# A graph layer with a mixture of experts: router and experts in one block, late buffers over the node rows, one semaphore per gathered tile

## The chip, the cores and the metric

The kernel runs on one core of a Trainium2 chip. The metric is the device time of one execution in microseconds (us), the median of several runs. The core's engines each run their own instruction stream and meet at semaphores: TensorE (PE) multiplies matrices, VectorE (DVE) and ScalarE (ACT) work on elements, GpSimd (POOL) does elementwise work and issues the DMAs whose rows are addressed by an index (gathers and scattered stores), and SyncE (SP) issues the other DMAs.

## The reference

6250 nodes of 256 features, 200,000 edges, 8 experts with a hidden width of 1024.

```python
xn = layernorm(x)
x = x + relu(gcn(xn, src, dst)) + linear_attention_block(xn)
h = layernorm(x)
probs = softmax(h @ gate_w + gate_b)
idx = argmax(probs)                     # one expert a node
pos = rank of the node among those of its expert, in node order
kept = pos < 977                        # capacity ceil(1.25 * 6250 / 8)
y = relu(h @ w1[idx] + b1[idx]) @ w2[idx] + b2[idx]
x = x + nan_to_num(y * prob * kept, nan=0, posinf=1e4, neginf=-1e4)
```

## The kernel before

The program is a sequence of blocks; each engine has one stream per block, and all engines meet in a barrier between two blocks.

1. `prepare` and `aggregate_and_mix`: the normalisation, the products with the graph weights, the gathering of one row an edge through GpSimd, the attention and its feed-forward part. The node rows end in two buffers in SBUF, `acc` (49 blocks of 128 nodes, 260 columns) and `res` (49 blocks, 256 columns).
2. `route`: adds the two parts (`x2` on VectorE), scales the sum on ACT into `res` (`scale`), computes mean and variance of each row, the logits of the gate on TensorE (`transposes`, `logits`), the best expert, the place in it (`places`) and, by a product of one-hot matrices (`owners`), the node that owns each of the 8 x 8 x 128 slots. The 49 blocks go in five groups, `RB = [0, 12, 24, 36, 44, 49]`. While VectorE works on the blocks of one group, it does the steps of the group before in the gaps between blocks; `steps` says which step lies in which gap (`normal`, `choose`, `counted`, `probability`, `assign`). ACT does `copy`, `root`, `exponent` and `scale`. SP stores, for each group, the rows with four more columns (`rows_out` to `node_features`) and the plain rows to the output (`x2_out`), and waits for all of these at the end.
3. `experts`: eight experts, each with 977 slots, in `RT = 8` tiles of 128 rows, the last of 81. All weights and activations are split in a high part and a rest (`w1h`, `w1l`, `bTh`, `bTl`, ...), and each product is three products.

One expert in `experts` has two phases. In the **first phase** TensorE makes, for each of the `FT = 8` pieces of the hidden width and for each half of the rows, six matmuls `e_f` (L1837) in one of four PSUM banks. ACT writes the bias and the relu into `hbuf` (L1785), VectorE splits that into `hTh` (L1903) and `hTl` (L1905) and reduces w2 to its rest. In the **second phase** TensorE makes, for each tile t of rows, the two transposes `e_t` of tile t of the *next* expert (L1823) and then 24 matmuls `e_y` (L1850). Behind them, for tile t:

- VectorE adds the bias (`yb`, L1929), ACT multiplies by the probability (`yv`, L1800);
- VectorE in `classify`: `low`, `big`, `finite` (L1918 to L1920), which stand for -1e4, +1e4 and "is a number";
- GpSimd adds `low` and `big` (L1738);
- VectorE in `result`: `copy_predicated` puts `yv` over `low` where it's finite (L1893), waits until the store of tile t-2 has landed, since `oo` has two buffers, and then makes `oo` = `rows` times a column + `low` (L1896);
- GpSimd stores `oo` to its nodes (L1730).

VectorE runs `result(t-2)` and `classify(t-1)` behind `yb` of tile t; the last two tiles' results fall around the end of the phase, `result(7)` behind piece 1 of the next expert's first phase. GpSimd's stream is written out like this:

```python
pool.wait_ge(inf_ok, (e * RT + t) * 2 + 2)
nc.gpsimd.tensor_tensor(low[...], low[...], big[...], ALU.add).then_inc(pool_st, 1)
if t > 0:
    store(e, t - 1)
...
store(e, RT - 1)
if e + 2 < EXP:
    load_rows(e + 2)
```

`load_rows` (L1714) issues eight gathers, one a tile, into one of the two buffers of `rows`. ACT normalises the gathered rows (`normalise`, L1759, output `xe`), tile 0 of the next expert at the last but one piece of the first phase. There `wait_rows` waits on one semaphore for the eight gathers of the buffer together. ACT copies the transposed rows (`bTh`, L1767) and VectorE takes the rest (`bTl`). SP loads w1 of the next expert (L1687) once `w1l` is done, and w2 (L1690) once `w2l` is. Experts 2 to 5 run in a hardware loop of two turns, the others are written out.

## Time and profile before

| | |
|---|---|
| median of 3 runs | 3107.11 us (3103.48 to 3110.45) |
| profiled execution | 3119.13 us |
| its span in the profile | 3117.4 us |
| mean granted clock of TensorE, share of full speed | 0.708 |
| TensorE matmul (PE) busy | 1802.9 us, 58% |
| VectorE (DVE) busy | 1236.0 us, 40% |
| ScalarE (ACT) busy | 802.9 us, 26% |
| GpSimd (POOL) busy | 1744.9 us, 56% |

Most of the span belongs to the aggregation, in which GpSimd issues 1563 gathers of edge rows. So these shares are averages over stages with different limits, and say little about the last 570 us, which the change touches. There the stretches have to be read by themselves: a row of the windows gives the busy time of each engine in one stretch; a row of a timeline gives one instruction with its start, its duration, its output and inputs, and in brackets how long its engine stood idle before it and what released it. "issue" there means that nothing shown in the profile was waited for. Of a matmul group or a pair of transposes the timeline's start is that of the first one.

### The profile page before, as it was taken

How to read it: one execution, taken by the hardware profiler on the slowest of the kernel's cores; microseconds unless marked ns; L12 is line 12 of the kernel's file. 1: busy time of each engine (PE TensorE's matmuls, PEld its weight loads, DVE VectorE, ACT ScalarE, POOL GpSimd, SP SyncE). 2: the span in 40 equal slices, each digit the busy share in tenths (PEclk: the TensorE clock that was granted, in tenths of full speed). 3: DMA queues.
4: the chain of work that ended last, by engine and by line, in shares of the span. 5: the costliest groups of instructions: out<-in, count | busy, mean ns of one | idle time of the engine just before them, and what ended most of it. 6: DMA issues, size and time to landing. Idle time of an engine off the chain costs nothing. (4 is left out here: it accounts for less than half of the span.)

```text
span 3117.4 us, 35225 instructions
## 1 busy us (share of the span) xinstructions
PE 1802.9 (58%) x8976; PEld 1564.4 (50%) x8976; DVE 1236.0 (40%) x3292; ACT 802.9 (26%) x1561; POOL 1744.9 (56%) x1844
## 2 busy tenths in 40 slices
PE   3745666645555555655555555555533356878978
PEld 2634444434444454544545445444422255778867
DVE  3522322233433334333343333434322247666756
ACT  1411212212222222222322222222100014544433
POOL 5055555666666666666666666666666630444544
PEclk6867888866666666666666666666666555889989
DMA  6366666666666665656556565666666635322220
GB/s 177 130 206 203 208 203 171 170 182 173 176 178 178 172 172 168 180 169 173 167 168 180 168 173 168 179 181 177 172 184 184 183 108 165 114 74 57 69 76 12
DMA packets 185241, 495.17 MB, mean 159 GB/s; under 512 B 34488, under 2 KB 66068, under 8 KB 184938
## 3 DMA queue, kind: packets, MB, share of 16 engines
q0 software_dynamic: 133008, 426.42, 47.8%
q1 hardware_dynamic: 52058, 66.62, 6.5%
q8 instruction: 85, 1.39, 0.2%
q14 instruction: 90, 0.74, 0.1%
HBM read 461.89 MB, written 33.79 MB: 159 GB/s over the span
## 5 line engine op out<-in xcount | busy, mean ns | idle before, releaser
L762 POOL DMA_INDIRECT ring<-node_rows,src_chunk x1563 | 1482.1, 948 | 954.5 <-SPq L741 448.7
L800 PE MATMUL p_item<-ring,sel 128*128 x3512 | 848.0, 393 | 727.6 <-DVE acc L1047 483.9
L800 PEld LDWEIGHTS p_item<-ring,sel 128*128 128x128 f32 x3512 | 692.1, 276 | 827.6 <-issue 825.1
L1047 DVE TENSOR_TENSOR acc<-acc,p_item 128x256 f32 (+1 forms) x439 | 183.6, 418 | 586.4 <-remote 454.7
L1028 DVE SCALAR_TENSOR_TENSOR sel<-dst_chunk,nbase,p_col 128x512 fp32r<-128x512 f32 x439 | 325.7, 742 | 63.9 <-issue 55.5
L840 PE MATMUL p_g<-x1T,w1t_sb 128*128 128x128 f32 x392 | 100.7, 438 | 173.6 <-ACT x1T L953 137.0
L1052 DVE SCALAR_TENSOR_TENSOR kf<-p_q,ke 128x256 f32<-128x256 f32 x49 | 20.8, 425 | 444.9 <-ACT ke L986 381.8
L840 PEld LDWEIGHTS p_g<-x1T,w1t_sb 128*128 128x128 f32 x392 | 86.7, 326 | 188.0 <-ACT x1T L953 148.4
L1738 POOL TENSOR_TENSOR low<-low,big 128x256 f32<-128x256 f32 x64 | 65.1, 1018 | 200.3 <-DVE big L1919 200.3
L1850 PE MATMUL e_y<-w2h,hTh 128*128 128x256 f32 x512 | 153.6, 300 | 0.2 <-DVE hTl L1905 0.2
L1850 PE MATMUL e_y<-w2l,hTh 128*128 128x256 f32 x512 | 147.9, 289 | 0.0
L1850 PE MATMUL e_y<-w2h,hTl 128*128 128x256 f32 x512 | 147.6, 288 | 0.0
L1714 POOL DMA_INDIRECT rows<-node_features,slot_row x64 | 68.9, 1077 | 120.3 <-POOLq L1199 101.2
L953 ACT ACTIVATE x1T<-p_t,col_ln1b,col_ln1g 128x128 f32<-128x128 f32 x98 | 39.5, 453 | 304.7 <-remote 285.2
L867 PE MATMUL p_q<-wq_sb,xnT_m 128*128 128x512 f32 x196 | 109.2, 685 | 8.4 <-ACT xnT_m L930 8.4
L860 PE MATMUL p_t<-ident,xn_m 128*128 128x128 f32 x98 | 26.0, 356 | 150.2 <-ACT xn_m L926 108.1
L1501 ACT COPY xT_r<-r_t 128x512 f32<-128x512 f32 (+1 forms) x25 | 14.3, 574 | 353.0 <-PE r_t L1548 352.9
L1850 PEld LDWEIGHTS e_y<-w2h,hTh 128*128 128x128 f32 x512 | 102.1, 199 | 0.7 <-DVE hTl L1905 0.6
L1850 PEld LDWEIGHTS e_y<-w2l,hTh 128*128 128x128 f32 x512 | 102.0, 199 | 0.0
L1850 PEld LDWEIGHTS e_y<-w2h,hTl 128*128 128x128 f32 x512 | 101.5, 198 | 0.0
L1125 DVE SCALAR_TENSOR_TENSOR kf<-p_q,ke 128x256 f32<-128x256 f32 x49 | 20.8, 424 | 200.3 <-ACT ke L939 101.1
L1837 PE MATMUL e_f<-bTh,w1h 128*128 128x490 f32 (+1 forms) x256 | 99.2, 387 | 1.7 <-issue 1.7
(258 smaller groups left out, 3167.4 us busy)
## 6 DMA issues: line engine op xcount, KB each, us to landing
ring<-node_rows,src_chunk POOLq DMA_INDIRECT x1563
self_rows<-node_rows SPq DMA_DIRECT2D x49, 256.0 KB
node_rows<-halves SPq DMA_DIRECT2D x11, 1024.0 KB, 4.3
w1raw<-in_w SPq DMA_DIRECT2D x8, 1024.0 KB
w2raw<-in_w SPq DMA_DIRECT2D x8, 1024.0 KB
res<-in_x SPq DMA_DIRECT2D x7, 896.0 KB, 7.9
node_features<-acc SPq DMA_DIRECT2D x3, 1560.0 KB, 6.2
out_dram<-res SPq DMA_DIRECT2D x3, 1536.0 KB, 10.9
```

What stands on the lines that cost most here:

```text
L762: nc.gpsimd.indirect_dma_start(ring[:, c % RING // U, c % U, :], None, table, bass.IndirectOffsetOnAxis(src_chunk[:, c:c + 1], 0)).then_in ...
L800: mm = pe.matmul(p_item[i % PSLOT][:, 0:C], sel[:, i % SELR, u, :], rows[:, u, h * C:(h + 1) * C].bitcast(F32R), start=(u == 0 and h == 0) ...
L840: mm = pe.matmul(p_g[:, m, :], w1t_sb[:, a, m * P:(m + 1) * P], x1T[:, a, :], start=(a == 0), stop=(a == CH - 1))
L860: mm = pe.transpose(p_t[:, a, :], xn[:, a * P:(a + 1) * P], ident[:])
L867: mm = pe.matmul(p_kv, xnT[:, a, :], wq_sb[:, a, C:3 * C], start=(a == 0), stop=(a == CH - 1))
L953: nc.scalar.activation(x1T[:, a, :], p_t[:, a, :], ACT.Identity, scale=g["cols"]["ln1g"][:, a:a + 1], bias=g["cols"]["ln1b"][:, a:a + 1]). ...
L1028: nc.vector.scalar_tensor_tensor(sel[:, i % SELR, :, :], dst.rearrange("p (u e) -> p u e", e=1).broadcast_to([P, U, P]), nbase[:, bass.ds( ...
L1047: nc.vector.tensor_tensor(a, a, p_item[j % PSLOT][:, 0:C], ALU.add).then_inc(added, 1)
L1714: nc.gpsimd.indirect_dma_start(rows[0:r, e % 2, t, :], None, feats, bass.IndirectOffsetOnAxis(slot_row[0:r, k:k + 1], 0)).then_inc(gathere ...
L1738: nc.gpsimd.tensor_tensor(low[0:r, t % 2, :], low[0:r, t % 2, :], big[0:r, t % 2, :], ALU.add).then_inc(pool_st, 1)
L1837: mm = pe.matmul(p_f[c % 4][:, 0:NH[h]], w[:, a, j * P:(j + 1) * P], b[:, a, h * NH[0]:h * NH[0] + NH[h]], start=(q == 0), stop=(q == len( ...
L1850: mm = pe.matmul(p_y[t % 2][:, 0:C], h[:, j, t * P:(t + 1) * P], w[:, j, :], start=(q == 0), stop=(q == len(parts) - 1))
```

## The change

- `route` and `experts` become one function, `tail`, with one block and no barrier between them. The buffers that the experts need late (`hTh`, `hTl`, `w2h`, `w2l`, `hbuf`, `finite`, `low`, `big`, `total`, `oo`) are put over `acc` and `res` in SBUF, the other ones have a place of their own. The PSUM banks of the router are those of the experts.
- The scaled rows in `res` are what is stored to `node_features`, with three further columns in place of four: `acc` is no longer multiplied again in the experts. The group's rows now wait for `scale` as well. SP issues the loads of expert 0's w1, w2 and the bias at the start of the block, and `x2_out` of a group directly behind its `rows_out`. The casts of expert 0's w1 (`high_w1`, `low_w1`) are done within routing. `root` of a group stands ahead of the group's last `copy`, steps of VectorE lie in other gaps, and `const3` is waited for later.
- Each gathered tile of rows has its own semaphore (`gathered[t]` for even experts, `arrived[t]` for odd ones), and `normalise` waits for its own tile.
- `oo` = `low` + `rows` is now a second addition on GpSimd, behind a wait for the landing of the store of tile t-2. VectorE makes `total` = `yv` + `rows` in `classify` and copies it over `oo` where it is finite; behind that the tile is stored.
- One semaphore fewer in the attention (`t_rec`), and strides of `res` and `acc` by the new widths.

```diff
-ROW = C + 4
+ROW = C + 3
...
+        nodes_at = nc.sbuf_base
+        acc = sb("acc", [P, NBLK, C])
+        res = sb("res", [P, NBLK, ROW])
+        nodes_end = nc.sbuf_base
...
-            acc = sb("acc", [P, NBLK, ROW], st=mid)
-            res = sb("res", [P, NBLK, C], st=mid)
...
-            route(nc, sb, ps, sem, locals())
-        experts(nc, sb, ps, sem, locals())
+        tail(nc, sb, ps, sem, locals())
...
+        over = [g["nodes_at"]]
+        def late(name, shape, dt=F32):
+            at = -(-over[0] // 32) * 32
+            over[0] = at + 4 * int(np.prod(shape[1:]))
+            assert over[0] <= g["nodes_end"]
+            return nc.alloc_sbuf_tensor_at(name, shape, dt, offset=at)
+        hTh, hTl = late("hTh", [P, FT, RT * P], F32R), late("hTl", [P, FT, RT * P], F32R)
+        w2h, w2l = late("w2h", [P, FT, C], F32R), late("w2l", [P, FT, C], F32R)
+        hbuf = late("hbuf", [P, 2, CAPE])
+        finite = late("finite", [P, 2, C], I32)
+        low, big = late("low", [P, 2, C]), late("big", [P, 2, C])
+        total, oo = late("total", [P, 2, C]), late("oo", [P, 2, C])
...
+        p_l, p_in, p_map = p_f[0:2], p_f[2:4], p_y[0]
...
+        arrived = [sem(f"arrived{t}", st) for t in range(RT)]
...
+        def wait_rows(eng, e, u, t):
+            if u == 0:
+                wait_apart(eng, gathered[t], rows_gathered(t) + e * 8 + 16, dma_fb, 32)
+            else:
+                wait_apart(eng, arrived[t], e * 8 + 8, dma_fb, 32)
...
+            def rows_out(gi):
+                sp.wait_ge(cols_ok, 3 * gi + 3)
+                sp.wait_ge(scaled, RB[gi + 1])
+                sp.dma_start(feats[RB[gi] * P:RB[gi + 1] * P, :].rearrange("(b p) c -> p b c", p=P),
+                             res[:, blocks(gi), :]).then_inc(dma_out, 16)
...
+            load_w1(sp, 0)
+            load_w2(sp, 0)
+            sp.dma_start(fb2_b[:].rearrange("p e c -> p (e c)"),
+                         fb2.rearrange("(a e) c -> a (e c)", a=1).broadcast_to([P, EXP * C])).then_inc(dma_fb, 16)
+            for gi in range(NG):
+                rows_out(gi)
+                x2_out(gi)
...
-            for gi in range(NG):
-                rows_out(gi)
-                if gi > 0:
-                    x2_out(gi - 1)
-            x2_out(NG - 1)
-            sp.wait_ge(dma_out, 16 * NOUT)
...
+            def load_rows(e):
+                for t in range(RT):
+                    r, k = nrows(t), e * RT + t
+                    nc.gpsimd.indirect_dma_start(
+                        rows[0:r, e % 2, t, :], None, feats, bass.IndirectOffsetOnAxis(slot_row[0:r, k:k + 1], 0)
+                        ).then_inc((gathered if e % 2 == 0 else arrived)[t], 16)
+            pool.wait_ge(slots_ok, 2)
+            pool.wait_ge(dma_out, 16 * NOUT)
...
+                pool.wait_ge(o_ok, k + 1)
...
+                    pool.wait_ge(inf_ok, T * 2 + 2)
+                    nc.gpsimd.tensor_tensor(low[0:r, t % 2, :], low[0:r, t % 2, :], big[0:r, t % 2, :], ALU.add
+                                            ).then_inc(pool_st, 1)
+                    pool.wait_ge(pool_st, T * 2 + 1)
+                    wait(pool, sent[t % 2], T // 2 * 16)
+                    nc.gpsimd.tensor_tensor(oo[0:r, t % 2, :], low[0:r, t % 2, :], rows[0:r, e % 2, t, 0:C], ALU.add
+                                            ).then_inc(pool_st, 1)
+                    if t > 0:
+                        store(e, t - 1)
+                store(e, RT - 1)
+                if e + 2 < EXP:
+                    load_rows(e + 2)
...
-                    V.scalar_tensor_tensor(acc[:, w, C], mv[:, :, 0], -1.0, r, ALU.mult, ALU.mult
+                    V.scalar_tensor_tensor(res[:, w, C], mv[:, :, 0], -1.0, r, ALU.mult, ALU.mult
                                            ).then_inc(cols_ok, 1)
+                    V.tensor_tensor(res[:, w, C + 1], r, sqd[:, w], ALU.mult).then_inc(cols_ok, 1)
...
+                    v.wait_ge(const3, 9)
...
-                for i, k in enumerate((0, 4, 4, 5, 5, 6)):
+                for i, k in enumerate((0, 5, 5, 6, 6, 7)):
...
-                for i, k in enumerate((17, 17, 18, 18, 19, 20, 21, 22)):
+                for i, k in enumerate((20, 20, 21, 21, 22, 22, 23, 23)):
...
-            v.wait_ge(const3, 9)
-            chain(V.tensor_copy(acc[:, :, C + 3:C + 4].rearrange("p b a -> p (b a)"), dinv[:]))
...
+                    v.wait_ge(pool_st, T * 2 + 2)
+                else:
+                    both = v.to_reg(T * 2 + 2)
+                    v.wait_ge(dma_fb, 32)
+                    v.wait_ge(fin_ok, both)
+                    v.wait_ge(pool_st, both)
+                V.copy_predicated(oo[0:r, t % 2, :], finite[0:r, t % 2, :], total[0:r, t % 2, :]
+                                  ).then_inc(o_ok, 1)
...
+                    V.tensor_tensor(total[0:r, t % 2, :], yv[0:r, t % 2, :], rows[0:r, u, t, 0:C], ALU.add
+                                    ).then_inc(fin_ok, 1)
...
+                    if gi == 1 and u < PC:
+                        low_w1(0, u)
...
+                wait_rows(s, e, u, t)
...
+                    if i == len(pairs(gi)) - 1:
+                        root(gi)
                     copy(t)
                     if i == 1 and gi > 0:
                         exponent(gi - 1)
-                    if 1 <= t <= held:
+                    if t > 0:
                         scale(t - 1)
-            root(NG - 1)
+                    if gi == 0 and i in (3, 4):
+                        high_w1(0, 2 * i - 6)
...
+                if t > 0:
+                    high_rows(0, t - 1)
+            high_rows(0, RT - 1)
+            s.wait_ge(dma_fb, 32)
+            s.wait_ge(dma_out, 16 * NOUT)
+            all_experts(s, expert)
...
-                elif t == 0:
-                    wait_rows(s, e, u)
...
-                V.copy_predicated(low[0:r, t % 2, :], finite[0:r, t % 2, :], yv[0:r, t % 2, :]).then_inc(o_ok, 1)
-                wait_apart(v, o_ok, 2 * T + 1, dma_fb, 16)
-                wait_apart(v, sent[t % 2], (e * (RT // 2) + t // 2) * 16, dma_fb, 16)
-                V.scalar_tensor_tensor(oo[0:r, t % 2, :], rows[0:r, u, t, 0:C], rows[0:r, u, t, C + 3:C + 4],
-                                       low[0:r, t % 2, :], ALU.mult, ALU.add).then_inc(o_ok, 1)
```

## Rows read from the trace of the kernel before

**Rows 1.** Windows: length, busy PE, PEld, DVE, ACT, POOL, PEclk, DMA, GB/s

```profile
2547.00:2644.00 97.00, 71.43 (x400) 68.30 (x400) 77.29 (x299) 47.45 (x93) 0.32 (x2) 0.50 0.37 124
3023.00:3032.00 9.00, 0.13 (x2) 0.11 (x2) 0.88 (x1) 0.78 (x2) 2.40 (x3) 0.65 0.67 171
```

**Rows 2.** TensorE timeline, experts: start, duration, instruction, [wait before it]

```profile
2690.09 0.38 PE L1823 MATMUL e_t<-ident,xe 128*128 128x128 f32 x2
...
2743.74 0.66 PE L1823 MATMUL e_t<-ident,xe 128*128 128x128 f32 x2 [6.78 <-issue]
...
2943.41 0.39 PE L1837 MATMUL e_f<-bTh,w1h 128*128 128x490 f32 x1
...
2974.58 0.68 PE L1823 MATMUL e_t<-ident,xe 128*128 128x128 f32 x2 [9.73 <-ACT xe L1759]
...
3031.92 0.66 PE L1823 MATMUL e_t<-ident,xe 128*128 128x128 f32 x2 [8.87 <-issue]
```

**Rows 3.** Timeline of ACT, the same columns

```profile
2973.85 0.60 ACT L1759 ACTIVATE xe<-rows 128x256 f32<-128x256 f32 x1 [10.89 <-DMA rows<-node_features,slot_row]
```

**Rows 4.** Timeline of GpSimd, the same columns

```profile
2648.50 0.97 POOL L1714 DMA_INDIRECT rows<-node_features,slot_row  x1 [101.18 <-POOLq L1199]
...
2940.48 1.00 POOL L1730 DMA_INDIRECT out_dram<-oo,slot_node  x1 [0.16 <-issue]
2942.66 0.73 POOL L1738 TENSOR_TENSOR low<-low,big 128x256 f32<-128x256 f32 x1 [1.18 <-DVE big L1919]
...
2949.17 1.28 POOL L1738 TENSOR_TENSOR low<-low,big 81x256 f32<-81x256 f32 x1 [0.73 <-DVE big L1919]
...
2955.12 1.77 POOL L1730 DMA_INDIRECT out_dram<-oo,slot_node  x1 [2.76 <-DVE oo L1896]
2957.19 1.06 POOL L1714 DMA_INDIRECT rows<-node_features,slot_row  x1 [0.30 <-issue]
...
2967.23 0.98 POOL L1714 DMA_INDIRECT rows<-node_features,slot_row  x1 [0.31 <-issue]
...
2988.92 1.03 POOL L1730 DMA_INDIRECT out_dram<-oo,slot_node  x1 [0.17 <-issue]
...
3093.94 1.01 POOL L1730 DMA_INDIRECT out_dram<-oo,slot_node  x1 [2.15 <-DVE oo L1896]
...
3107.81 1.24 POOL L1730 DMA_INDIRECT out_dram<-oo,slot_node  x1 [0.16 <-issue]
...
3112.12 1.01 POOL L1730 DMA_INDIRECT out_dram<-oo,slot_node  x1 [0.57 <-issue]
```

**Rows 5.** Timeline of VectorE, the same columns

```profile
2547.35 0.21 DVE L1460 COPY acc<-dinv 128x49 f32<-128x49 f32 x1 [1.89 <-POOL node_hi L1262]
...
2945.57 0.49 DVE L1896 SCALAR_TENSOR_TENSOR oo<-rows,low 128x256 f32<-128x256 f32 x1 [1.17 <-DMA out_dram<-oo,slot_node]
...
2949.20 0.66 DVE L1903 CAST hTh<-hbuf 128x978 fp32r<-128x978 f32 x1
...
2993.15 0.48 DVE L1896 SCALAR_TENSOR_TENSOR oo<-rows,low 128x256 f32<-128x256 f32 x1 [0.27 <-DVE low L1893]
...
3110.73 0.48 DVE L1896 SCALAR_TENSOR_TENSOR oo<-rows,low 81x256 f32<-81x256 f32 x1
```

**Rows 6.** The chain that ended last, from 2974 us on: start, length, work

```profile
3001.77 21.28 PE e_f L1837 x96
...
3059.05 21.29 PE e_f L1837 x96
```

**Rows 7.** Timeline of SP's DMA queue, the columns of the timelines

```profile
2639.48 1.89 SPq L1275 DMA_DIRECT2D out_dram<-res  x2
...
2647.84 0.39 SPq L1687 DMA_DIRECT2D w1raw<-in_w  x1
...
2939.91 0.37 SPq L1687 DMA_DIRECT2D w1raw<-in_w  x1
```

More of the change, by code:

```diff
@@ new lines, in tail @@
+        hTh, hTl = late("hTh", [P, FT, RT * P], F32R), late("hTl", [P, FT, RT * P], F32R)
[4 more added lines that the diff above has]
+        total, oo = late("total", [P, 2, C]), late("oo", [P, 2, C])
+        p_t = [ps(f"e_t{i}", [P, 4, P], st) for i in range(2)]
+        p_f = [ps(f"e_f{i}", [P, 512], st) for i in range(4)]
@@ new lines, in tail @@
+        p_y = [ps(f"e_y{i}", [P, 512], st) for i in range(2)]
+        p_l, p_in, p_map = p_f[0:2], p_f[2:4], p_y[0]
+        (const3, mean_ps, centred, x2_ok, var_ok, std, cols_ok, turned, xT_ok, l_ps, dv, e_ok, e_act, oh_ok, cum, one_ok, mapped,
+         scaled, slots_ok) = (sem("r_" + n, st) for n in (
+            "const3", "mean", "centred", "x2", "var", "std", "cols", "turned", "xT", "lps", "dv", "e", "eact", "oh", "cum", "one",
+            "mapped", "scaled", "slots"))
+        d_w1, d_w2 = sem("d_w1", st), sem("d_w2", st)
@@ L1237, in route @@
+        arrived = [sem(f"arrived{t}", st) for t in range(RT)]
+        sent = [sem(f"e_sent{i}", st) for i in range(2)]
+        (xe_ok, tr_ok, bh_ok, bl_ok, f1_ps, r_ok, hi_ok, lo_ok, f2_ps, yb_ok, y_ok, pool_st, inf_ok, fin_ok, o_ok,
+         w1h_ok, w1l_ok, w2h_ok, w2l_ok) = (sem("e_" + n, st) for n in (
+            "xe", "tr", "bh", "bl", "f1", "r", "hi", "lo", "f2", "yb", "y", "pool", "inf", "fin", "o", "w1h", "w1l",
+            "w2h", "w2l"))
         block = st.enter_context(nc.Block())
@@ L1249, in blocks_of, with nrows, w1_piece, w2_piece @@
             return range(2 * t, min(2 * t + 2, NBLK))
+        def nrows(t):
+            return P if t < RT - 1 else LASTR
+        def w1_piece(w, q):
+            n = F * CH // PC
+            return w[:, q * n // F, q * n % F:q * n % F + n]
+        def w2_piece(w, q):
+            return w[:, q * FT // PC:(q + 1) * FT // PC, :]
+        def all_experts(eng, expert):
+            for e in range(2):
+                expert(e, e, True)
+            with eng.Fori(1, EXP // 2 - 1) as it:
+                for u in range(2):
+                    expert(it * 2 + u, u, True)
+            expert(EXP - 2, 0, True)
+            expert(EXP - 1, 1, False)
@@ new lines, in rows_gathered, with load_w1 @@
+        def rows_gathered(t):
+            units = range(t, NUNIT, RING // U) if t < RING // U else ()
+            return 16 * sum(min(U, NCHUNK - k * U) for k in units)
+        def wait_rows(eng, e, u, t):
[3 more added lines that the diff above has]
+                wait_apart(eng, arrived[t], e * 8 + 8, dma_fb, 32)
+        def load_w1(sp, e):
+            sp.dma_start(w1raw[:], w1[bass.ds(e, 1)].rearrange("e (k p) f -> p (e k) f", p=P)).then_inc(d_w1, 16)
@@ new lines, in _, with store @@
+            load_rows(1)
+            def store(e, t):
+                r, k = nrows(t), e * RT + t
+                pool.wait_ge(o_ok, k + 1)
+                nc.gpsimd.indirect_dma_start(
+                    out, bass.IndirectOffsetOnAxis(slot_node[0:r, k:k + 1], 0), oo[0:r, t % 2, :], None,
+                    bounds_check=N - 1, oob_is_err=False).then_inc(sent[t % 2], 16)
+            for e in range(EXP):
+                for t in range(RT):
+                    r = nrows(t)
+                    T = e * RT + t
+                    pool.wait_ge(inf_ok, T * 2 + 2)
[10 more added lines that the diff above has]
+                    load_rows(e + 2)
@@ L1285, in _ @@
+            for q in range(2):
+                pool.wait_ge(sent[q], 16 * EXP * RT // 2)
         @block.vector
@@ new lines, in high_rows, with high_w1, high_w2 @@
+            def high_rows(e, t):
+                r = nrows(t)
+                s.wait_ge(tr_ok, e * RT + t + 1)
+                nc.scalar.copy(bTh[:, :, t * P:t * P + r], p_t[t % 2][:, 0:CH, 0:r]).then_inc(bh_ok, 1)
+            def high_w1(e, q):
+                if q == 0:
+                    s.wait_ge(d_w1, e * 16 + 16)
+                nc.scalar.copy(w1_piece(w1h, q), w1_piece(w1raw, q)).then_inc(w1h_ok, 1)
+            def high_w2(e, q):
+                if q == 0:
+                    s.wait_ge(d_w2, e * 16 + 16)
+                    wait(s, f2_ps, e * RT)
+                nc.scalar.copy(w2_piece(w2h, q), w2_piece(w2raw, q)).then_inc(w2h_ok, 1)
@@ new lines, in expert @@
+            def expert(e, u, more):
+                for j in range(FT):
+                    for h in range(2):
+                        wait_apart(s, f1_ps, e * 2 * FT + 2 * j + h + 1, dma_fb, 32)
+                        wait_apart(s, lo_ok, e * FT + j - 1, dma_fb, 32)
+                        nc.scalar.activation(hbuf[:, j % 2, h * NH[0]:h * NH[0] + NH[h]],
+                                             p_f[(2 * j + h) % 4][:, 0:NH[h]], ACT.Relu,
+                                             bias=fb1_sb[:, bass.ds(e, 1), j]).then_inc(r_ok, 1)
+                    if 1 <= j < 1 + PC:
+                        high_w2(e, j - 1)
+                    if more and j == FT - 2:
+                        normalise(e + 1, 1 - u, 0)
+                for t in range(RT):
+                    r = nrows(t)
+                    if more:
+                        high_rows(e + 1, t)
+                        if t + 1 < RT:
+                            normalise(e + 1, 1 - u, t + 1)
+                    s.wait_ge(yb_ok, e * RT + t + 1)
+                    wait(s, o_ok, e * RT + t - 1)
+                    nc.scalar.activation(yv[0:r, t % 2, :], yb[0:r, t % 2, :], ACT.Identity,
+                                         scale=rows[0:r, u, t, C + 2:C + 3]).then_inc(y_ok, 1)
+                    if more and 1 <= t < 1 + PC:
+                        high_w1(e + 1, t - 1)
```

460 lines of the change are left out of this document (151 added, 309 removed).

## The prediction, made before the result was known

> **What bounds the kernel now.** I read the windows first, then TensorE's timeline, then those of ACT, GpSimd, VectorE and SP. The aggregation fills the first 2547 us; the diff leaves its order of work alone (one semaphore fewer in `attention`, other strides), so I give it no change. Routing takes about 97 us, and VectorE is its busiest engine with 77.3 of them [rows 1]. Then come the barrier, the first gather at 2648.50 [rows 4] and the experts, to the end.
>
> In `experts` TensorE sets the pace: per expert a first phase of 96 matmuls `e_f` (21.3 us [rows 6]) and a second of eight tiles of `e_y`. Call F the start of the second phase, its first `e_t`. F is 2690.09 for expert 0, 2743.74 for the next, 2974.58 for expert 5, 3031.92 for expert 6 [rows 2] and 3080.34 for expert 7 (3059.05 + 21.29 [rows 6]). Six periods from 2690.09 to 3031.92 are 57.0 us each; the seventh is 48.4. The six end in a wait of TensorE in front of `e_t`, 6.78 us in the first, 9.73 and 8.87 in the last two [rows 2]; the seventh has none, and the difference of 8.6 is its price. What is late? ACT's `normalise` of tile 0 waits 10.89 us for DMA `rows` [rows 3]. The chain behind it: `result(e,7)` on VectorE, the expert's last store at 2955.12, eight gathers from 2957.19 to 2967.23, and the landing, at 2973.85 (6.6 us after the last one's start) [rows 3, 4]. `normalise` of tile 0 waits on one semaphore for all eight. While TensorE stands still its granted clock falls, to a mean of 0.65 in that window [rows 1].
>
> **Part 1, a semaphore per gathered tile.** Tile 0's gather starts 10.04 us before tile 7's [rows 4]. With the same 6.6 it lands at 2963.8; `e_f` ended at 2974.58-9.73 = 2964.85. If nothing before it is later, the whole wait goes, 8.6 a period. The other tiles start some 1.4 us apart and are used 27.2/8 = 3.4 apart, so they aren't late.
>
> **Part 2, the second GpSimd addition.** Here the change gives back. Before, VectorE wrote `oo`, and the wait for the landing of store t-2 stood there, two tiles later and mostly covered. VectorE gets `total` in `classify` instead, an addition of the same size (0.48 [rows 5]), so its own sum stays. Now GpSimd does low(t), waits for `sent` (store t-2 landed), adds `oo`, starts store(t-1). Store t-2 is the instruction just ahead of low(t), so its landing lies wholly in a loop: a turn = landing, counted from the store's start, + addition 0.73 + gap 0.16 [rows 4]. A landing isn't shown, so it is bounded. VectorE was held until 2945.57, 5.09 after the store at 2940.48 [rows 4, 5], but SP had started a `w1raw` load 0.57 us before that store [rows 7]. In the last expert, where no load runs, `oo` went at 3110.73 without such a wait, 2.92 after the store at 3107.81: there it's at most 2.9. In the middle experts `oo`(2) went at 2993.15, 4.23 after store(0) at 2988.92, held by another thing [rows 4, 5]: at most 4.2. From below, a turn can't be shorter than its own work: low, `oo` and store, 0.73+0.73+1.03+gaps 0.5 = 3.0 [rows 4]. I take 2.9 for a quiet landing (turn 3.8), one of four like it in that expert, and 5.0 for the one store of an expert beside the `w1` load (turn 5.9).
>
> The Trainium skill, "DMA: Bandwidth & Descriptors" (the table of fixed and variable cost), puts a DMA at about 2.0 us and bytes/436e9: an estimate of 2.3 us for 128 KB, 3.3 with 1.0 of issue, so turns of 3.2 to 4.2; with the middle of it the sum would stay the same. No run here shows the split.
>
> One middle expert, from F. (VectorE's and ACT's small steps are 0.3 to 0.6 each, like those of [rows 3, 5].) Store(0) started at 2988.92 = F+14.3. Ahead of it VectorE loses `oo`, 0.48 and a gap of 0.27 [rows 5]; GpSimd gains 0.89: s0 = F+14.5, and the turns give s1 = 18.3, s2 = 22.1, s3 = 25.9, s4 = 31.8 (contended: the load starts about F+24), s5 = 35.6.
> - Second phase: `e_t`(7) needs `xe`(7), which ACT issues behind yv(5), result(3), oo(3); that is done at s2-0.2 = 21.9. With copy_predicated, yv, bTh and xe, 2.2 together: 24.1, and `e_y`(7) ends at 27.4. Before: 3001.77-2974.58 = 27.2 [rows 2, 6]. So +0.2.
> - First phase: ACT reaches `hbuf`(0) behind yv(7), result(5), oo(5), done at 31.6: 33.4. TensorE has filled its four banks at 27.4+5.3 = 32.7 and waits 0.7. VectorE reaches `hTh`(0) behind oo(6) = 35.4, copy_predicated and `classify`(7): 37.0, which is 9.6 after the phase began, against 5.8 before (2949.20-2943.41 [rows 2, 5]). `hTl`(0) is ready at 38.9, `hbuf` of j=2 at 39.8; TensorE wanted it at 38.7: 1.1. Afterwards the engines keep step as now. Sum +1.9: 23.2, end at 50.6.
> - Gathers: oo(7), store(6) and store(7) behind s5, at the slow rate of the first phase (addition 1.28, store 1.77 [rows 4]): first gather at about 43.6, landed at 50.2. No wait, with 0.4 us to spare.
>
> With VectorE's `hTl`(7) 0.4 behind, the period is 51.0 for 57.0: six times -6.0, **-36**. Expert 6 to 7 had no wait to lose: 48.4 becomes 49.5, **+1.1**. In the last expert the tiles end by the loop: store(0) was at F+13.6, of which 2.15 is a stray gap [rows 4], so s0 = F+12; six turns 22.8, result(7) and a clash 1.4, and the 5.3 from the last store's start to the end (3112.12 to 3117.4): 41.5 for 37.1, **+4.7** with part of the gap kept.
>
> **Part 3, one program.** The `const3` wait ahead of routing goes: VectorE idled 1.89 before 2547.35 [rows 5], **-1.4**. At the end of routing two `out_dram` stores went out from 2639.48 to 2641.4, SP got past the barrier at 2647.84 and GpSimd gathered at 2648.50 [rows 4, 7]. The store of group 3 now leaves earlier, the last one 1.9 us earlier, and no barrier stands behind it; GpSimd still waits for all of `dma_out`. First gather near 2645: **-3.5**. Expert 0's `w1`: SP issues three loads at its start, ACT gets four casts, VectorE four subtractions, 0.6 to 0.7 each, under routing, where VectorE idled 19.7 of 97 us [rows 1]; uncovered 5.2. `e_f` then doesn't wait for the last `w1l` piece: **-1.6**. `root` now stands ahead of the last copy of a group and holds it until the variances are ready; later gaps for `assign` may save VectorE its waits for TensorE. Both together 0, bounds -5 and +5.
>
> **Sum.** -6.5 - 36 + 1.1 + 4.7 = -36.7. The profiled execution took 3119.13 (span 3117.4 and 1.7 around it): 3082.4. The median of the runs was 3107.11, so 3070.
>
> **Rivals.**
> - The loop costs more, slower: quiet landing 4.2, turn 5.1, five such turns an expert, +6.5 us that all come through. Period 57.5: six times +0.5; seventh +9; last +13; front -4. Together +21: 3128. It decides from a landing of 3.9. For it: the distance of 4.23 in the middle experts excludes no less. Against: 2.92 in the last.
> - The loop is covered: landing 2.2 or less, turns near 3.1 to 3.6. Period 48.7, -50; front -13 with VectorE's waits gone; last +2: 3046.
> - Port clashes: low beside `hTh` and `hTl` took 1.28 for 0.73 [rows 4]. Five additions now fall in the first phase; if each stops VectorE for its 0.73, +3.6 an expert: the saving is 2.4 x 6, seventh +4.7, the rest as above, 3095. The Trainium skill, "SBUF — State Buffer" (Who interferes with whom), has a VectorE instruction with two SBUF inputs and a GpSimd one that reads SBUF block each other fully. By that rule, the stretched row agrees.
> - The change doesn't do what it says: tile 0 lands as late as tile 7, no wait goes; 3107 with a covered loop.
>
> **How the numbers follow.** Forecast 0.55 (3050 to 3088), slow loop 0.17, covered loop 0.13, clashes 0.11, nothing gained 0.04. The range 3042 to 3108 leaves out the slow loop and little more. A measurement of this kernel can tell about 0.2% from no change, 6.2 us. Faster 0.77, same 0.07, slower 0.16.
>
> **What would show it.** No 7 to 10 us ahead of `e_t` of tile 0, and no fallen clock there; GpSimd's `oo` addition waiting for DMA `out_dram`, released 2.9 after the store, once an expert near 5; copy_predicated waiting for GpSimd; 23 us of `e_f`. I am wrong if the landing isn't 2.9, or if first gathers come after F+46.

## The result

The changed kernel takes 3064.95 us (median of 4 runs, 3060.90 to 3071.16) where the kernel before took 3108.78 in the same runs: a ratio of 0.9861, 95% interval 0.9836 to 0.9886. That is 43.8 us less. The forecast was 3070, the range 3042 to 3108.

The profiled execution took 3060.90 us, its span is 3059.1 us: 58.3 less than the profile of before. Not all of this is the change's. The aggregation's last step on VectorE stands at 2545.04 us in the profile of before and here at

```profile
2533.93 0.42 DVE L1048 TENSOR_TENSOR acc<-acc,p_item 128x256 f32<-128x256 f32 x1 [0.46 <-PE p_item L801]
```

11.1 us earlier, in a stage that the change leaves alone. In the ten profiles of the experiments, whose kernels all share this stage, it stands anywhere from 2529.45 to 2549.33 in eight runs on two chips, and at 2104.5 and 2105.0 in two runs on a third. On the first two chips and here, its mean is 2538.6 us in the three profiles of kernels with the old routing and 2538.3 in the seven with the new one: it is scatter. So below I use **the tail**: the span less that time. It is 572.4 us before and 525.2 after, 47.2 less, close to what the medians say. For a single profile it tells more than the span.

TensorE's timeline of the changed kernel, the start of a second phase (the first `e_t`) for experts 0, 1, 5 and 6, as [rows 2]:

```profile
2667.28 0.38 PE L1892 MATMUL e_t<-ident,xe 128*128 128x128 f32 x2
...
2716.52 0.44 PE L1892 MATMUL e_t<-ident,xe 128*128 128x128 f32 x2 [0.30 <-DVE w2l L1603]
...
2917.79 0.43 PE L1892 MATMUL e_t<-ident,xe 128*128 128x128 f32 x2 [0.43 <-DVE w2l L1603]
...
2967.65 0.44 PE L1892 MATMUL e_t<-ident,xe 128*128 128x128 f32 x2 [0.36 <-DVE w2l L1603]
```

The waits of 6.78 to 9.73 us of [rows 2] are gone, 0.3 to 0.5 are left. Six periods take 50.06 us each ((2967.65-2667.28)/6). What the windows show of the granted clock behind the wait was not in my sum. Six microseconds of the second phase of experts 3, 4 and 5 before (the columns of [rows 1]; the sixth figure after the stretch's length is the granted clock):

```profile
2860.00:2866.00 6.00, 5.70 (x30) 5.71 (x31) 2.19 (x3) 2.04 (x5) 0.00 (x0) 0.56 0.01 3
2916.00:2922.00 6.00, 5.70 (x35) 5.71 (x36) 2.61 (x4) 2.10 (x6) 0.00 (x0) 0.68 0.00 0
2974.00:2980.00 6.00, 5.42 (x34) 5.42 (x35) 2.61 (x4) 2.33 (x5) 0.00 (x0) 0.68 0.00 0
```

and of the changed kernel, experts 3, 4 and 5:

```profile
2817.00:2823.00 6.00, 5.16 (x41) 4.96 (x42) 4.41 (x6) 1.85 (x5) 3.66 (x4) 1.00 0.95 244
2867.00:2873.00 6.00, 5.02 (x40) 4.74 (x40) 4.67 (x7) 1.82 (x5) 3.92 (x4) 1.00 0.87 263
2917.00:2923.00 6.00, 4.93 (x39) 4.38 (x38) 4.76 (x7) 2.00 (x4) 4.24 (x4) 1.00 0.77 154
```

Before, TensorE came out of its wait at half clock (1.2 GHz; behind the first wait the window 2743 to 2749 reads 0.50 throughout) and got the full 2.4 GHz only some microseconds later: 30 to 35 matmuls in 6 us in these three. Now the clock is at 1.00 at the start of every second phase, and TensorE does 39 to 41 in the same time although it still pauses for `hTl`. It falls once more, in the middle of expert 6's second phase (see the seventh period below).

GpSimd's timeline of the changed kernel, middle of expert 4, as [rows 4]:

```profile
2880.92 1.29 POOL L1391 DMA_INDIRECT out_dram<-oo,slot_node  x1 [0.17 <-issue]
...
2885.05 1.02 POOL L1391 DMA_INDIRECT out_dram<-oo,slot_node  x1 [0.16 <-issue]
2886.27 0.73 POOL L1400 TENSOR_TENSOR low<-low,big 128x256 f32<-128x256 f32 x1 [0.21 <-DVE big L1642]
2887.64 0.76 POOL L1404 TENSOR_TENSOR oo<-low,rows 128x256 f32<-128x256 f32 x1 [0.63 <-DMA out_dram<-oo,slot_node]
2888.56 1.00 POOL L1391 DMA_INDIRECT out_dram<-oo,slot_node  x1 [0.16 <-issue]
...
2892.14 1.00 POOL L1391 DMA_INDIRECT out_dram<-oo,slot_node  x1 [0.16 <-issue]
2893.35 0.73 POOL L1400 TENSOR_TENSOR low<-low,big 128x256 f32<-128x256 f32 x1 [0.21 <-DVE big L1642]
2897.00 0.74 POOL L1404 TENSOR_TENSOR oo<-low,rows 128x256 f32<-128x256 f32 x1 [2.92 <-DMA out_dram<-oo,slot_node]
2897.89 1.00 POOL L1391 DMA_INDIRECT out_dram<-oo,slot_node  x1 [0.15 <-issue]
...
2908.56 1.74 POOL L1391 DMA_INDIRECT out_dram<-oo,slot_node  x1 [2.19 <-DVE oo L1619]
2910.60 1.06 POOL L1374 DMA_INDIRECT rows<-node_features,slot_row  x1 [0.30 <-issue]
```

This is the loop of part 2. A quiet store lands 2.59 us after its start (2885.05 to 2887.64), a turn is 3.5 (2885.05 to 2888.56); the one of 2892.14, beside the `w1` load that SP starts 0.58 before it, lands after 4.86, its turn is 5.75. In the last expert the turns are 3.3 to 3.6. SP's queue:

```profile
2891.56 0.37 SPq L1320 DMA_DIRECT2D w1raw<-in_w  x1
```

### The profile page after: what moved, and what is told of

Its sections match the earlier page's. It is cut to its first block and busy times, and to the rows that moved or that the text cites. A ratio compares the mean times of both kernels' runs of the same rounds, so it can differ in the third digit from the quotient of the medians.

```text
span 3059.1 us, 35293 instructions
## 1 busy us (share of the span) xinstructions
PE 1785.2 (58%) x8976; PEld 1547.8 (51%) x8976; DVE 1256.7 (41%) x3296; ACT 798.5 (26%) x1561; POOL 1788.8 (58%) x1908
## 5 line engine op out<-in xcount | busy, mean ns | idle before, releaser
L801 PE MATMUL p_item<-ring,sel 128*128 x3512 | 837.3, 390 | 653.8 <-DVE acc L1048 454.5
L801 PEld LDWEIGHTS p_item<-ring,sel 128*128 128x128 f32 x3512 | 684.3, 273 | 750.4 <-issue 747.5
L1053 DVE SCALAR_TENSOR_TENSOR kf<-p_q,ke 128x256 f32<-128x256 f32 x49 | 20.8, 425 | 506.9 <-ACT ke L987 324.3
L841 PE MATMUL p_g<-x1T,w1t_sb 128*128 128x128 f32 x392 | 99.1, 433 | 164.4 <-ACT x1T L954 147.6
L819 PE MATMUL p_q<-xnT_m,wq_sb 128*128 128x128 f32 x392 | 80.3, 371 | 126.3 <-ACT xnT_m L980 124.2
L819 PEld LDWEIGHTS p_q<-xnT_m,wq_sb 128*128 128x128 f32 x392 | 72.5, 277 | 132.0 <-ACT xnT_m L980 128.1
L861 PE MATMUL p_t<-ident,xn_m 128*128 128x128 f32 x98 | 25.9, 354 | 149.1 <-ACT xn_m L927 106.9
L1400 POOL TENSOR_TENSOR low<-low,big 128x256 f32<-128x256 f32 x64 | 52.0, 812 | 82.7 <-DVE big L1642 82.2
L1906 PE MATMUL e_f<-bTl,w1h 128*128 128x490 f32 (+1 forms) x256 | 99.5, 388 | 0.0
```

What stands on the lines that cost most here:

```text
L801: mm = pe.matmul(p_item[i % PSLOT][:, 0:C], sel[:, i % SELR, u, :], rows[:, u, h * C:(h + 1) * C].bitcast(F32R), start=(u == 0 and h == 0) ...
L819: mm = pe.matmul(p_q[:, m, :], wq_sb[:, a, m * P:(m + 1) * P], xnT[:, a, :], start=(a == 0), stop=(a == CH - 1))
L841: mm = pe.matmul(p_g[:, m, :], w1t_sb[:, a, m * P:(m + 1) * P], x1T[:, a, :], start=(a == 0), stop=(a == CH - 1))
L1400: nc.gpsimd.tensor_tensor(low[0:r, t % 2, :], low[0:r, t % 2, :], big[0:r, t % 2, :], ALU.add).then_inc(pool_st, 1)
L1906: mm = pe.matmul(p_f[c % 4][:, 0:NH[h]], w[:, a, j * P:(j + 1) * P], b[:, a, h * NH[0]:h * NH[0] + NH[h]], start=(q == 0), stop=(q == len( ...
```

## The experiments

All times are medians against runs of the kernel before on the same chip; "tail" is from the profile, as above (before 572.4). Experiments 1 to 4 ran on one chip (the kernel before: 3108.41 us), 5 to 8 on a second (3111.22), 9 and 10 on a third (2679.18). The periods and tails are from one profile each.

**1. Part 1 alone.** The kernel before, with

```diff
-                        ).then_inc(gathered[t] if e == 0 else d_r[e % 2], 16)
+                        ).then_inc((gathered if e % 2 == 0 else arrived)[t], 16)
...
-                elif t == 0:
-                    wait_rows(s, e, u)
+                wait_rows(s, e, u, t)
```

> The kernel before with part 1 alone (a semaphore for each gathered tile, and the attention's two semaphores merged as in the change, to make room). Theory: the wait ahead of `e_t` cost more than its 8.6 us, since TensorE's granted clock stood at 0.57 for the first 6 us of the second phase behind it; without it the second phase is as short as that of expert 0 (25.5 us of `e_y` for 27.5) and the first keeps its 21.4. Periods of 47.0 us for 57.0, six of them, and the seventh 47 for 48.4: -61 in all, 3047 us, so faster than the changed kernel. Rival: tile 0's gather starts some 41 us behind the start of the second phase and lands 5 us later, when TensorE is already through: a wait of 1 to 2 us stays and the periods are 49, 3060.

Measured 3044.61 us against 3108.41, ratio 0.9782 (0.9758 to 0.9805); tail 512.5. Six periods of 47.2, the seventh 46.7, the last expert 36.2. TensorE doesn't wait, and the windows at the start of the second phases of experts 1 and 4:

```profile
2734.00:2740.00 6.00, 5.99 (x50) 5.70 (x49) 4.11 (x6) 2.71 (x6) 3.22 (x3) 1.00 0.86 257
...
2875.00:2881.00 6.00, 5.62 (x44) 5.20 (x43) 4.67 (x7) 2.04 (x4) 4.02 (x4) 1.00 0.88 264
```

The second phases of experts 1 to 6 take 155.7 us together, for 164.4 in the kernel before. A period is 9.75 shorter (56.97 and 47.22): 8.7/6 = 1.45 of it is the second phase behind the fallen clock, 8.3 the wait, for which I had read 8.6. One part of the change gives more than the whole of it. The rival's rest of a wait isn't there.

**2. Part 2 undone in the changed kernel.**

```diff
-                    wait(pool, sent[t % 2], T // 2 * 16)
-                    nc.gpsimd.tensor_tensor(oo[0:r, t % 2, :], low[0:r, t % 2, :], rows[0:r, e % 2, t, 0:C], ALU.add
-                                            ).then_inc(pool_st, 1)
...
-                V.copy_predicated(oo[0:r, t % 2, :], finite[0:r, t % 2, :], total[0:r, t % 2, :]
-                                  ).then_inc(o_ok, 1)
+                V.copy_predicated(low[0:r, t % 2, :], finite[0:r, t % 2, :], yv[0:r, t % 2, :]).then_inc(o_ok, 1)
+                wait_apart(v, o_ok, 2 * T + 1, dma_fb, 32)
+                wait_apart(v, sent[t % 2], (e * (RT // 2) + t // 2) * 16, dma_fb, 32)
+                V.tensor_tensor(oo[0:r, t % 2, :], rows[0:r, u, t, 0:C], low[0:r, t % 2, :], ALU.add).then_inc(o_ok, 1)
...
-                    V.tensor_tensor(total[0:r, t % 2, :], yv[0:r, t % 2, :], rows[0:r, u, t, 0:C], ALU.add
-                                    ).then_inc(fin_ok, 1)
```

> The changed kernel with part 2 undone: GpSimd adds only `low` and `big`, VectorE copies over `low` and adds `rows` into `oo` behind its own wait for the landing of the store of tile t-2. Theory (the loop on GpSimd costs 2 us of each first phase and 3.7 at the end): periods of 47 for 50, the last expert 37 for 40.8: 3 x 7 + 4 = 25 less than the changed kernel, 3040 us. Rival: the time behind the second phase is lost to the two engines' clashes in `hTh` and `hTl`, which VectorE's `oo` brings back in another form: 5 to 8 less, 3058.

Measured 3036.98 us, ratio 0.9761 (0.9737 to 0.9784); tail 500.1. It is the lowest median on this chip, with an interval that overlaps those of experiments 1 and 3. First phases 21.5, six periods 47.3, last expert 36.2. In the middle experts the chain that ended last now runs through TensorE; two of its pieces:

```profile
2795.16 21.35 PE e_f L1902 x96
...
2870.55 2.90 PE e_y L1915 x24
```

In the changed kernel the same chain goes through the landings of the stores, here in expert 4:

```profile
2885.05 2.46 DMA out_dram<-oo,slot_node
2888.56 2.44 DMA out_dram<-oo,slot_node
2892.14 4.72 DMA out_dram<-oo,slot_node
2897.89 2.38 DMA out_dram<-oo,slot_node
```

**3. Four buffers for `oo`.** GpSimd keeps both additions; it waits for the store four tiles back.

```diff
-                    wait(pool, sent[t % 2], T // 2 * 16)
+                    wait(pool, sent[t % 4], T // 4 * 16)
```

> The changed kernel with four buffers for `oo` and four `sent` semaphores (two pairs of others merged to make room): GpSimd still makes both additions, but waits for the store four tiles back. Theory (what costs is the landing in the loop): the turns fall from 3.5 and 5.75 us to TensorE's 3.1, the first phase goes from 23.6 to 22, the last expert from 40.8 to 38: 17 less than the changed kernel, 3048 us. Rival (what costs is GpSimd's second addition itself, and VectorE stopped beside it): turns as before but for the one beside the load, at most 5 less, 3060.

Measured 3040.41 us, ratio 0.9776 (0.9750 to 0.9802); tail 504.1. First phases 21.5, six periods 47.1, last expert 37.5. So the cost was the landing in the loop: with it out, the addition on GpSimd gives the same periods as that on VectorE (47.1 and 47.3), and I had expected too little of it (3048). Of the 4 us more in the tail than in experiment 2, 2.8 stand ahead of expert 0's second phase. GpSimd's timeline in the last expert has turns of 3.0 us (3023.59 to 3026.58), the lower end of my bound:

```profile
3023.59 1.25 POOL L1395 DMA_INDIRECT out_dram<-oo_b,slot_node  x1 [0.15 <-issue]
...
3026.58 1.24 POOL L1395 DMA_INDIRECT out_dram<-oo_a,slot_node  x1 [0.16 <-issue]
```

**4. The changed kernel again.**

> The changed kernel once more, on the chip of the others, as the measure for them: 3065 us. Its trace also shows how much the aggregation varies: its last step on VectorE ended 11.1 us earlier than in the kernel before, though the change alters nothing there but strides and one semaphore; I expect values spread over 10 us for either kernel.

Measured 3066.13 us, ratio 0.9866 (0.9840 to 0.9892); tail 525.9, periods 50.15, the aggregation's end at 2529.76. Experiment 2 is 29 us faster (26 in the tail): this is what part 2 costs. By the forecast's own terms it was 2.5 a period, 1.1 and 4.7, 21 in all; here it is 2.9 a period, 2.8 in the seventh and 5.3 in the last.

**5. Part 1 undone.** `normalise` of tile 0 waits for all eight tiles of its expert.

```diff
-                wait_rows(s, e, u, t)
+                if isinstance(e, int) and e == 0:
+                    wait_rows(s, e, u, t)
+                elif t == 0:
+                    for every in range(RT):
+                        wait_rows(s, e, u, every)
```

> The changed kernel with part 1 undone: `normalise` of tile 0 waits for the eight gathers (experts 1 to 7). Theory: the wait is back and longer than before the change, since the first gather starts 43.1 us behind the start of the second phase (before the change 40.9) and the last one 10 later: periods of 59.2 to 60 for 50.1, with a granted clock below 0.7 at the start of the second phase: 3120 to 3127 us, slower than the kernel before. Rival: the per-tile semaphores did nothing, the wait went by the rest of the change: 3065.

Measured 3129.65 us against 3111.22, ratio 1.0056 (1.0033 to 1.0080); tail 587.0. Periods of 59.9, as foretold, and a granted clock of 0.50 to 0.70 over the 6 us behind the waits; the time is 3 us above what I had expected. TensorE's timeline has the waits again, here those of experts 2 and 5; the second was 9.73 in [rows 2]:

```profile
2802.78 0.68 PE L1896 MATMUL e_t<-ident,xe 128*128 128x128 f32 x2 [9.79 <-ACT xe L1740]
...
2983.19 0.69 PE L1896 MATMUL e_t<-ident,xe 128*128 128x128 f32 x2 [10.57 <-ACT xe L1740]
```

**6. The next w1 loaded later**, when the stores of the second phase have gone out.

```diff
-                    sp.wait_ge(w1l_ok, e * PC + PC)
+                    if isinstance(e, int) and e == 0:
+                        sp.wait_ge(w1l_ok, PC)
+                    else:
+                        sp.wait_ge(o_ok, e * RT)
                     load_w1(sp, e + 1)
```

> The changed kernel with the load of the next w1 held until the last `copy_predicated` of the expert before (for experts 1 to 6), so that no store of the second phase runs beside it. Theory: the fifth turn of 5.75 us (landing 4.9) becomes 3.5 like the others, the stores from s4 on are 2.2 earlier, ACT reaches `hbuf` 2 us earlier: 1.5 a period, 10 us in all, 3055. Rival: that landing is long for another reason and the time doesn't move; or the load now meets the gathers and `xe` waits for them, then slower by 1 to 2 a period.

Measured 3057.64 us, ratio 0.9828 (0.9802 to 0.9855); tail 515.9, that is 10 less than in experiment 4 (525.9), periods of 48.4. (By the medians it is 8.5 less, with intervals that overlap a little.) GpSimd's timeline at the store that took 4.86 to land:

```profile
2893.91 1.00 POOL L1394 DMA_INDIRECT out_dram<-oo,slot_node  x1 [0.16 <-issue]
2895.12 0.73 POOL L1403 TENSOR_TENSOR low<-low,big 128x256 f32<-128x256 f32 x1 [0.21 <-DVE big L1645]
2896.48 0.74 POOL L1407 TENSOR_TENSOR oo<-low,rows 128x256 f32<-128x256 f32 x1 [0.64 <-DMA out_dram<-oo,slot_node]
```

2.57 us, like the others. The load beside it was the reason.

**7. The store ahead of the addition.** Two lines moved on GpSimd.

```diff
+                    if t > 0:
+                        store(e, t - 1)
                     pool.wait_ge(pool_st, T * 2 + 1)
                     wait(pool, sent[t % 2], T // 2 * 16)
                     nc.gpsimd.tensor_tensor(oo[0:r, t % 2, :], low[0:r, t % 2, :], rows[0:r, e % 2, t, 0:C], ALU.add
                                             ).then_inc(pool_st, 1)
-                    if t > 0:
-                        store(e, t - 1)
```

> The changed kernel with one line moved on GpSimd: store(t-1) is started ahead of the wait for store(t-2) and of the addition `oo`(t). The landing now has two turns' time. Theory (a loop through both engines): the store's 1.0 us, which ran beside VectorE's copy_predicated and `classify`, now stands in the loop: addition 0.73, VectorE 1.2, `low` 0.73, store 1.0 and gaps 0.3, a turn of 4.0; six turns 24 against 23.3 as it is, so no change within 5 us, 3065. Rival (the landing alone costs): as with four buffers, 15 less, 3050.

Measured 3081.39 us, ratio 0.9919 (0.9890 to 0.9948); tail 541.6: 15 to 16 us slower than the changed kernel. Both expectations missed the number; GpSimd's timeline shows the mechanism of the first:

```profile
2894.40 1.02 POOL L1391 DMA_INDIRECT out_dram<-oo,slot_node  x1 [0.16 <-issue]
2895.42 0.67 POOL L1406 TENSOR_TENSOR oo<-low,rows 128x256 f32<-128x256 f32 x1
2897.13 1.05 POOL L1400 TENSOR_TENSOR low<-low,big 128x256 f32<-128x256 f32 x1 [1.04 <-DVE big L1642]
2898.34 1.26 POOL L1391 DMA_INDIRECT out_dram<-oo,slot_node  x1 [0.16 <-issue]
```

The wait for the landing is gone, and GpSimd waits 1.04 for VectorE instead: a turn of 3.9 to 4.2. But I set 24 for six turns against 23.3 and forgot the one beside the load, which stays at 5.3 here. Store 0 to store 6 takes 25.3 us for 23.7 in the changed kernel, 1.6 a period; the period is 51.5 for 50.1. Of the 15.7 us by which the tail is longer than in experiment 4, 8.3 lie in the six periods, 2.9 in the seventh, 2.9 in the last expert and 1.5 ahead of expert 0's second phase.

**8 and 9. Work in TensorE's wait.** The kernel before with matmuls whose result is overwritten, between the two phases, 48 of them for experts 1 to 6, then 50 for expert 1 and 66 for the others.

```diff
+                    if more and t == 0 and not (isinstance(e, int) and e == 0):
+                        t_.wait_ge(yb_ok, e * RT)
+                        for q in range(48):
+                            pe.matmul(p_y[0][:, 0:C], w1h[:, 0, 0:P], bTh[:, 0, 0:C], start=(q == 0), stop=(q == 47))
                     if more:
                         transposes(e + 1, t)
```

> The kernel before, with 48 matmuls of 128x256 more (some 6.2 us at full clock, their result is overwritten) on TensorE between the first and the second phase of experts 1 to 6, in the time in which it waits for the gathered rows. The wait itself stays where it ended. Theory: what TensorE does before the second phase keeps its granted clock at 1.0, and the 6 us in which it stood at 0.57 become full ones: 1.5 to 2 us less a period, 10 less in all, 3098, with more work done. Rival: the slow start of the second phase belongs to something else (rows that come late from ACT and VectorE): no gain, 3108.

Measured 3107.69 us against 3111.22, ratio 0.9997 (0.9977 to 1.0016): no difference that this run can tell. In the profile the tail is 565.2, 7 less, and the six second phases take 158.2 us for 164.4.

> As the run with 48 matmuls, but 66 of them (8.1 us) ahead of the second phase of experts 2 to 6 and 50 for expert 1. In the run with 48 the first 6 us of the second phase ran at a granted clock of 1.00 in the three experts where TensorE then waited about 1 us more, and at 0.72 to 0.98 where it waited 3 us or more. Theory: now no wait over 2 us is left, the clock is at 1.00 at the start of each second phase, and the six second phases take 25.6 to 26.2 us for 27.0 to 27.9 before: 1.6 x 6 = 9 less, 1.6 given back in expert 4, whose wait is shorter than the work put in; 7 less, 3104. Rival: as many second phases at 27 as in the run with 48; then it isn't the length of the wait that lets the clock fall.

This ran on the third chip, where the kernel before takes 2679.18 us: measured 2672.99, ratio 0.9977 (0.9968 to 0.9987), 6 us faster with 380 matmuls more. The six second phases take 156.7 us for 164.4 before. Windows at their start in experts 1 and 2, and the `e_t` that starts each:

```profile
2303.00:2309.00 6.00, 5.43 (x44) 5.23 (x45) 3.03 (x5) 3.51 (x8) 0.00 (x0) 1.00 0.00 0
2362.00:2368.00 6.00, 6.00 (x39) 6.00 (x40) 2.61 (x4) 2.25 (x6) 0.00 (x0) 0.72 0.00 0
```

```profile
2303.42 0.44 PE L1823 MATMUL e_t<-ident,xe 128*128 128x128 f32 x2 [0.84 <-ACT xe L1759]
...
2361.88 0.43 PE L1823 MATMUL e_t<-ident,xe 128*128 128x128 f32 x2 [2.59 <-ACT xe L1759]
```

A pause of 0.84 us leaves the clock at full, one of 2.59 doesn't. In the six experts here it held at four (pauses of 0.84, 1.47, none and 1.45) and fell at two (2.59 and 1.93); with 48 matmuls it held at three, one of them behind a pause of 3.10, which my expectation overlooked. In these two profiles a second phase takes 25.5 to 25.9 us where the clock held (seven of them) and 26.9 to 27.1 where it fell (five). So the clock's fall is a part of the wait's price, shown; the length of the last pause alone doesn't settle when it falls, and my expectation that none would fall was wrong.

**10. Two loads beside the first gathers.** In the changed kernel, w2 of expert 0 and w1 of expert 1 are held until GpSimd gathers.

```diff
-            load_w2(sp, 0)
...
+            sp.wait_ge(slots_ok, 2)
+            sp.wait_ge(dma_out, 16 * NOUT)
+            load_w2(sp, 0)
```

> The changed kernel with two of SP's loads (w2 of expert 0, w1 of expert 1, 1 MB each) held until GpSimd starts its first gathers. Theory: in the kernel before, the first gather landed 7.0 us after its start, beside three loads, in the changed one 2.84, and this is 4.2 of the 11.7 us by which expert 0's second phase is earlier. So the landing is back near 6 to 7 us, expert 0's second phase starts 3 to 4 us later against the end of the aggregation (133.4 in the changed kernel): 137, and the time is 3069. Rival: what shortened it is w1's casts being done already: 133.4 as it is, 3065.

Third chip: 2633.17 us against 2679.18, ratio 0.9836 (0.9822 to 0.9850), 46.0 less; tail 526.8, against 525.2 and 525.9 for the changed kernel. The first gather started at 2201.85 and ACT got its rows only 6.72 us later, as foretold; but the rows of the other tiles were there by then, and from then on ACT's timeline has a tile each 0.85 us:

```profile
2208.57 0.60 ACT L1738 ACTIVATE xe<-rows 128x256 f32<-128x256 f32 x1 [13.43 <-DMA rows<-node_features,slot_row]
...
2210.29 0.60 ACT L1738 ACTIVATE xe<-rows 128x256 f32<-128x256 f32 x1
...
2211.12 0.60 ACT L1738 ACTIVATE xe<-rows 128x256 f32<-128x256 f32 x1
```

Expert 0's second phase starts 134.6 us after the aggregation's end; in the seven other profiles of kernels with part 3 it is 133.4 to 136.2. Counted from the first gather it is 37.3 us, for 35.7 to 37.7 in those seven and 41.6 in the kernel before. So the late landing costs nothing that stands out of this scatter, and the time is on the rival's side; that it is w1's casts that count isn't shown by this run alone.

## Why the prediction came out

The time is right within 5 us and the mechanisms are those that it names; that it is so close is in part luck, since two errors of size ran against each other. The terms, from the two profiles (F as in the prediction):

| | forecast | measured |
|---|---|---|
| aggregation | 0 | -11.1, scatter |
| its end to expert 0's F | -6.5 | -11.7 (145.05 to 133.35) |
| six periods | 6 x -6.0 (51.0) | 6 x -6.9 (50.06) |
| seventh period | +1.1 | +2.5 (50.75) |
| last expert | +4.7 | +3.5 |
| sum without the aggregation | -36.7 | -47.2 |

**Part 1** takes the wait away, some 8.3 a period for the 8.6 of the prediction; experiments 1 and 5 show it by adding and by removing it. The mis-sized term is the second phase. I took over its 27.2 us and came to 27.4; it is 26.2. Those 27.2 held the slow matmuls behind the wait. So did the seventh period, which I read as free of the wait and took as the measure: its second phase, 27.0 us, began behind a wait of 8.87. Only expert 0's began behind none, and it took 25.4 in the kernel before. I had cited the fallen clock in the wait's own window [rows 1] and not looked at the window after it. Experiment 9 shows in the time, and both 8 and 9 in their windows, that keeping TensorE at work brings part of it back.

**Part 2** gives back what was forecast, by the loop that was forecast, with a somewhat shorter landing: 2.59 for 2.9, a turn of 3.5 for 3.8; beside the load 4.86 for 5.0, a turn of 5.75 for 5.9. Store 0 came at F+13.5 for 14.5, the first gather at F+43.1 for 43.6. The first phase is 23.6 for 23.2: VectorE starts `hTh`(0) 9.1 us into it (forecast 9.6), and ACT's `hbuf`(0) holds TensorE for 1.3 us in expert 0. Experiments 2, 3, 6 and 7 change the loop in four ways, and the periods follow the turns in each (in 7 the cost was 15 us where I had foretold none). The trace agrees with the estimate drawn from the page "DMA: Bandwidth & Descriptors" of the Trainium skill, 2.3 us for a quiet store, within 0.3.

**The slow loop** was the rival on the other side; it needed a landing of 3.9. The 4.23 us of [rows 4, 5] were another thing's wait, and only the last expert's 2.92 bounded the landing. **Port clashes**: they exist. Where VectorE's `total` and GpSimd's `low` addition start together, one of the two is stretched: in the first pair below `total` takes 0.99 and `low` its 0.74, in the second `total` takes 0.41 and `low` 1.04. The last row is a `total` with no addition of GpSimd beside it, 0.42. This agrees with what the Trainium skill's page "SBUF — State Buffer" (Who interferes with whom) says of a VectorE instruction with two SBUF inputs beside a GpSimd one that reads SBUF. But experiment 3 keeps these clashes and has the shortest periods, 47.1 for the 47.3 of experiment 2: they cost nothing that the periods show where VectorE has slack. From the timelines of the changed kernel:

```profile
2879.13 0.74 POOL L1400 TENSOR_TENSOR low<-low,big 128x256 f32<-128x256 f32 x1 [1.80 <-DVE big L1642]
2879.17 0.99 DVE L1645 TENSOR_TENSOR total<-yv,rows 128x256 f32<-128x256 f32 x1
...
2882.80 1.04 POOL L1400 TENSOR_TENSOR low<-low,big 128x256 f32<-128x256 f32 x1 [0.59 <-DVE big L1642]
2882.83 0.41 DVE L1645 TENSOR_TENSOR total<-yv,rows 128x256 f32<-128x256 f32 x1
...
2982.74 0.42 DVE L1645 TENSOR_TENSOR total<-yv,rows 128x256 f32<-128x256 f32 x1
```

**The seventh period** was forecast +1.1 and is +2.5 or, in experiment 4, +1.6. The +1.1 has no working; the prediction's own terms for one period (+0.2, +1.9 and +0.4) give +2.5. In both profiles GpSimd started store 0 of expert 6 1.89 us late without a cause that the profile shows, and TensorE then waited 1.86 and 1.87 us for `xe` of tile 6. What differs is the clock behind this wait. Windows of the changed kernel and, in the second row, of experiment 4:

```profile
2989.00:2993.00 4.00, 3.65 (x19) 3.65 (x20) 3.68 (x9) 1.57 (x4) 2.43 (x4) 0.59 0.16 54
2986.00:2990.00 4.00, 3.88 (x33) 3.88 (x34) 3.69 (x9) 1.34 (x4) 2.40 (x3) 1.00 0.11 37
```

It fell in the one and not in the other, behind a wait of the same length, and the second phase of expert 6 took 29.4 us in the one and 27.9 in the other. A wait inside a phase can cost the same slow matmuls as one ahead of it.

**Part 3** is worth 12.4 us in the tail (512.5 and 500.1, experiments 1 and 2) for the 6.5 forecast. Two terms were too small. The first gather stands 96.5 us behind the aggregation's end for 103.5, -7.0 where -4.9 was forecast. Up to the last store to `node_features` it is 89.6 for 94.0, -4.4 where I had -1.4 and put `root` and the other gaps at 0; which of them gave the 3.0 stays open. From that store to the first gather it is 6.9 for 9.4, -2.5 for the forecast -3.5. From there to the second phase it is 36.8 for 41.6, -4.7 where I had -1.6 for the last piece of w1. I had priced the wait of TensorE alone (1.66 us ahead of the first `e_f` in the kernel before); on ACT the four casts of w1 stood between the tiles' copies too. ACT's timeline of the kernel before has 1.28 us a tile there:

```profile
2660.38 0.60 ACT L1759 ACTIVATE xe<-rows 128x256 f32<-128x256 f32 x1
...
2661.14 0.62 ACT L1772 CAST w1h<-w1raw 128x512 fp32r<-128x512 f32 x1
2661.66 0.60 ACT L1759 ACTIVATE xe<-rows 128x256 f32<-128x256 f32 x1
```

In the changed kernel the casts are gone, but a tile still takes ACT 1.2 to 2.1 us, because the rows land no faster; only in experiment 10, where the first rows came as late as in the kernel before, does one see its pace without casts, 0.85. By that experiment the other candidate, the loads beside the gathers, isn't what made the difference; no run puts the casts back, so that they are the cause is argued from these rows. By the medians part 3 is 7.6 us (3044.61 and 3036.98), with intervals that overlap.

In all, a forecast of -37 met -47 in the tail and -44 in the medians. By the tails part 1 gave 59.9 for the 51.6 of the forecast (6 x 8.6), part 3 12.4 for 6.5, together 14 more; part 2 cost 25.1 (525.2 and 500.1) for 20.8, 4 more. The two errors ran against each other.

## What to carry to other kernels

Read what a wait costs in the window behind it too: where TensorE stood still, its matmuls went on at half clock for microseconds, and a period that begins behind such a wait is no measure of one without it. When work is moved to an engine that also starts the stores, look at whether the wait for a landing moves with it into a loop; a second pair of buffers was worth nearly as much as moving the work back (3040 and 3037 against 3066). And where a stage that isn't touched scatters by 20 us, compare from its end, not from the start.
